# VectorE's copy of the turned rows, moved within its step in the graph layers and in the first phase

## The chip, the cores and the metric

The kernel runs on one core of one Trainium2 chip. Its time is the device time of one execution in microseconds (us). Five engines work side by side, each through its own instructions in order: TensorE (PE in the profile, with its weight loads as PEld), VectorE (DVE), ScalarE (ACT), GpSimd (POOL) and SyncE (SP). They wait for each other through semaphores.

## The reference

There are 10,000 nodes with rows of 512 numbers, and 10,000 edges sorted by their target node. The rows are normalized, go through three layers of a graph network, are added back, and go through a mixture-of-experts block with eight experts.

```python
h = layernorm(x)
for l in range(3):
    h_neigh = segment_sum(h[src], dst) / max(degree, 1)
    rst = relu(h @ W_self[l] + h_neigh @ W_neigh[l] + b[l])
    h = rst / max(norm(rst), 1e-12)
x = x + h
x = x + ffn(layernorm(x))      # top 2 of 8 experts, layer norm at the end
```

## The kernel before

Rows are worked in 79 tiles of 128. A neighbour sum is taken after the product: the kernel first computes y = h @ W_neigh and s = h @ W_self + b for every row, writes both to memory, and the next layer gathers rows of y by `src`, sums them by `dst` with a one-hot matrix on TensorE and adds s. So the work has four stages: a first phase (normalize x, multiply with the weights of layer 0), layer 1 and layer 2 (aggregate, normalize, multiply with the next weights), and a last stage (aggregate, then the expert block), which the change does not touch. The first phase also prepares the weights of all layers and the tables that place edges and nodes; that work is put between the tiles at fixed steps.

A product is made more exact by splitting h into a high part and a low part, both in 16 bits: `HH[i][:, 0, :]` is written by ScalarE (`hi0`, line 832; `hhi`, line 876), `HH[i][:, 1, :]` is the rest and is written by VectorE (line 1191; `hlo`, line 1346). TensorE turns both parts (`turn`, line 1613: eight 128 by 128 transposes into `psT`), VectorE copies them to SBUF (`turn`, line 1199, `HT`), and TensorE multiplies: `neigh` into `psY` and `own` into `psS`, twelve matmuls each (line 486). ScalarE and VectorE take y from `psY` as a high and a low part (`yhi`, line 841; `ylo`, line 1206), and VectorE takes s (`sev`, line 1216, `SB`).

The order on each engine is a list of stages with offsets: `(1, turn)` in step t means tile t+1. A step of TensorE in a layer is `neigh(t)`, `turn(t+1)`, `own(t)`, `aggregate(t+3)`; in the first phase it is the same without `aggregate`. `neigh(t)` waits for the copy of tile t (`s.ht`), and `turn(t)` waits for both parts of tile t. `HT`, `HH`, `psT`, `psY` and `psS` have two buffers each.

A step of VectorE in a layer is `one_hot(t+5)` (line 1298, `Sm`), `hlo(t+2)`, `ylo(t)`, `turn(t+1)`, `carry_lo(t+3)` (line 1307, the carry of a sum from one tile of edges to the next), `combine(t+3)` (line 1322, `R`), `sum_squares(t+3)` (line 1330), `sum_floor(t+3)` (line 1340), `sev(t)`. ScalarE computes the high part of the carry (line 857) as soon as `aggregate` is done. GpSimd raises the sum of squares to the power -1/2 (`scl`, line 728; line 656 in the first phase), and ScalarE's `hhi` uses it. GpSimd also issues the indirect transfers (lines 633, 706, 719, 735), each in its order.

In the first phase a step of VectorE is `norm0(t+2)`, `ylo(t)`, `turn(t+1)`, `stats0(t+3)`, `sev(t)`, with the preparation work ahead of `norm0`. `norm0` writes the normalized row `R` (line 1187), then waits for ScalarE's high part and writes the low part (line 1191), two instructions in one function.

Of the kernel before, what the change touches and what calls it, by code (L numbers as in the profile page):

```python
# [23 lines left out]
T = -(-E // EPT)  # L24
# [76 lines left out]
def run_steps(tiles, stages, begin, end, run=0):  # L101
    for step in range(begin, end):
        for off, f in stages:
            if 0 <= step + off < tiles:
                f(Tile(step + off, run))


def run_tiles(tiles, stages, run=0):
    offs = [o for o, _ in stages]
    run_steps(tiles, stages, -max(max(offs), 0), tiles - min(min(offs), 0), run)  # L110


def run_plan(tiles, stages, jobs, windows=()):
    offs = [o for o, _ in stages]
    begin, end = -max(max(offs), 0), tiles - min(min(offs), 0)
    cuts = sorted({begin, end} | {j[0] for j in jobs} | {e for w in windows for e in w[:2]})
    for a, b in zip(cuts, cuts[1:]):
        for at, f, arg in jobs:
            if at == a:
                f() if arg is None else f(arg)  # L120
        run_steps(tiles, stages + [(0, f) for x, y, f in windows if x <= a and b <= y], a, b)


def after(eng, sem, n):
    if n > 0:
        eng.wait_ge(sem, n)
# [101 lines left out]
def build(nc, x, src, dst, W_self, W_neigh, b, Wg, W1, b1, W2, b2, ln_g, ln_b, out_g, out_b, out):  # L228
    with ExitStack() as ctx:
# [733 lines left out]
        def _(dve):  # L963
# [218 lines left out]
            def norm0(t):  # L1182
                i = t.slot(2)
                dve.wait_ge(s.sc, (t + 1).n)
                after(dve, s.hhi, (t + -1).n)
                after(dve, s.hlo, (t + -1).n)
                dve.tensor_scalar(R[i][:, :], X[i][:, :], mv[:, i, 0:1], scl[:, i:i + 1], ALU.subtract, ALU.mult  # L1187
                                  ).then_inc(s.rr, 1)
                dve.wait_ge(s.hhi, (t + 1).n)
                dve.wait_ge(s.rr, (t + 1).n)  # L1190
                dve.scalar_tensor_tensor(HH[i][:, 1, :], R[i][:, :], LN_UP, HH[i][:, 0, :], ALU.mult, ALU.subtract  # L1191
                                         ).then_inc(s.hlo, 1)

            def turn(t, l):
                s = ph[l]
                i = t.slot(2)
                dve.wait_ge(s.tr, (t + 1).n)
                after(dve, s.sp, (t + -1).n)
                dve.tensor_copy(HT[i][:, :, :, :], psT[i][:, :, :, :]).then_inc(s.ht, 1)  # L1199

            def ylo(t, l):
                s = ph[l]
                i = t.slot(2)
                dve.wait_ge(s.yhi, (t + 1).n)
                k = Y_LN / (WUP * LN_UP) if l == 0 else Y_H / (WUP * H_UP)
                dve.scalar_tensor_tensor(YB[i][:, D:2 * D], psY[i][:, :], k, YB[i][:, 0:D], ALU.mult, ALU.subtract  # L1206
                                         ).then_inc(s.ylo, 1)

            def sev(t, l):
                s = ph[l]  # L1210
                i = t.slot(2)
                dve.wait_ge(s.sp, (t + 1).n)
                if t.t >= 2:
                    dve.wait_ge(s.s2[i], (t + -2).landed(2))
                c = C[f"s{l}"]
                dve.scalar_tensor_tensor(SB[i][:, :], psS[i][:, :], downs[:, c:c + 1], bias[:, l, :],  # L1216
                                         ALU.mult, ALU.add).then_inc(s.sev, 1)
# [44 lines left out]
            def tables():  # L1262
# [6 lines left out]
                for l in range(LAYERS):  # L1269
# [4 lines left out]

            rest = range(N_FIRST, len(NAMES))
            run_plan(TN,
                     [(2, norm0), (0, lambda t: ylo(t, 0)), (1, lambda t: turn(t, 0)), (3, stats0),
                      (0, lambda t: sev(t, 0))],
                     [(WSTEP(m) + 2, weight_norm, m) for m in rest] + [(WSTEP(m) + 3, weight_scale, m) for m in rest]
                     + [(WSTEP(m) + 4, weight_lo, m) for m in rest]  # L1280
# [12 lines left out]
            def one_hot(t, l):  # L1293

                s = ph[l]
                i = t.slot(GRING)
                after(dve, s.agg, (t + (1 - GRING)).n)
                dve.tensor_scalar(Sm[i][:, :], iota16[:, :], colT[:, t.t:t.t + 1], rowval[:, 0:1],
                                  ALU.is_equal, ALU.mult).then_inc(s.smat, 1)

            def carry_lo(t, l):
                s = ph[l]
                i, o = t.slot(2), (t + 1).slot(GRING)
                if t.t == T - 1:
                    return
                dve.wait_ge(s.chi, (t + 1).n - t.run)
                dve.scalar_tensor_tensor(G[o][0:1, D:2 * D], psA[0 if l == 3 else i][0:1, :], 1.0 / CARRY,
                                         G[o][0:1, 0:D], ALU.mult, ALU.subtract).then_inc(s.clo, 1)

            def combine(t, l):  # L1310
                s = ph[l]
                i = t.slot(2)
                if l == 1:
                    dve.wait_ge(s.x[i], t.landed(2))
                else:
                    dve.wait_ge(s.xs[i], Tile(t.t, l - 2).landed(2))
                dve.wait_ge(s.agg, (t + 1).n)
                if l == 3 and not (t.t == T - 1):

                    dve.wait_ge(s.chi, (t + 1).n - t.run)  # L1320
                after(dve, s.rr, (t + -1).n)
                dve.scalar_tensor_tensor(R[i][:, :], psA[0 if l == 3 else i][:, :], invs[:, l - 1, t.t:t.t + 1],  # L1322
                                         Sl[i][:, :], ALU.mult, ALU.add).then_inc(s.r, 1)

            def sum_squares(t, l):

                s = ph[l]
                i = t.slot(2)
                dve.wait_ge(s.r, (t + 1).n)
                dve.scalar_tensor_tensor(junk[:, :], R[i][:, :], 0.0, R[i][:, :], ALU.max, ALU.mult,  # L1330
                                         accum_out=ss[:, i:i + 1]).then_inc(s.dv2, 1)

            def sum_floor(t, l):

                s = ph[l]
                i = t.slot(2)
                dve.wait_ge(s.dv2, (t + 1).n)
                after(dve, s.sc, (t + -1).n)
                up = 1.0 if l == 3 else H_UP ** -2
                dve.tensor_scalar(ssm[:, i:i + 1], ss[:, i:i + 1], 1e-24, up, ALU.max, ALU.mult).then_inc(s.ss, 1)  # L1340

            def hlo(t, l):
                s = ph[l]
                i = t.slot(2)
                dve.wait_ge(s.hhi, (t + 1).n)
                dve.scalar_tensor_tensor(HH[i][:, 1, :], RR[i][:, :], scl[:, i:i + 1], HH[i][:, 0, :],  # L1346
                                         ALU.mult, ALU.subtract).then_inc(s.hlo, 1)

            for l in (1, 2):
                run_tiles(T, [(5, lambda t, l=l: one_hot(t, l)), (2, lambda t, l=l: hlo(t, l)), (0, lambda t, l=l: ylo(t, l)),  # L1350
                                      (1, lambda t, l=l: turn(t, l)), (3, lambda t, l=l: carry_lo(t, l)),
                                      (3, lambda t, l=l: combine(t, l)), (3, lambda t, l=l: sum_squares(t, l)),
                                      (3, lambda t, l=l: sum_floor(t, l)), (0, lambda t, l=l: sev(t, l))], l - 1)

# [407 lines left out]
```

## Time and profile before

| | us |
|---|---|
| median of 3 runs | 2334.58 (2333.9 to 2334.83) |
| the profiled execution | 2329.04 |
| its span, first to last instruction | 2327.3 |
| PE busy | 2108.8 (91%) |
| DVE busy | 1784.6 (77%) |
| POOL busy | 1253.7 (54%) |
| ACT busy | 990.4 (43%) |

The page of the profile gives the busy time of every engine, the chain of work that ended last, and the costliest groups of instructions. A matmul's end is modelled: consecutive matmuls overlap in the records, so the distance between two starts says more than a duration. Idle time of an engine is put down to the engine and line that released it.

### The profile page before, as it was taken

To read this page: it belongs to the slowest core of one execution; us is meant where nothing else is said; L and a number is where in the kernel's file an instruction comes from. 1 tells how busy PE (TensorE), PEld (TensorE's weight loads), DVE (VectorE), ACT (ScalarE), POOL (GpSimd) and SP (SyncE) were. 2 spreads that over 40 slices of the span, in tenths; PEclk is the share of its full clock that TensorE was granted. 3 is DMA by queue.
4 is the path that set the end of the run, shared out by engine and by line. 5 is a ranking of instruction groups with operands and counts; after the bars stand their busy time and mean duration, and the time that the engine had idled before them with its cause. 6 is when DMAs were issued, how large, how long until landed. Compare 5 with 4: busy or idle time off the path is not lost.

```text
span 2327.3 us, 45193 instructions
## 1 busy us (share of the span) xinstructions
PE 2108.8 (91%) x15947; PEld 1163.2 (50%) x15947; DVE 1784.6 (77%) x4201; ACT 990.4 (43%) x1698; POOL 1253.7 (54%) x1396
## 2 busy tenths in 40 slices
PE   1988889888799999999799999998389999999997
PEld 0444344334344444444344444444167777777775
DVE  4778887556587878887688787876479999999974
ACT  1222111111233333333333333332677777777761
POOL 3770003871455555554344444443658888888754
PEclk9999999999899999999899999999589999999998
DMA  4453335783355555554566666664546565565533
GB/s 129 138 153 120 109 118 132 116 114 107 121 170 163 168 167 170 163 168 144 167 206 209 211 210 205 209 212 165 158 108 143 129 138 136 129 138 135 132 49 43
DMA packets 162789, 343.48 MB, mean 148 GB/s; under 512 B 32153, under 2 KB 32327, under 8 KB 162567
## 3 DMA queue, kind: packets, MB, share of 16 engines
q0 software_dynamic: 60816, 165.43, 27.3%
q1 hardware_dynamic: 101751, 175.16, 25.5%
q8 instruction: 130, 2.13, 0.4%
q14 instruction: 92, 0.75, 0.1%
HBM read 175.81 MB, written 165.31 MB: 147 GB/s over the span
## 4 chain that ended last, share of the span: by engine, by line
PE 52%; DVE 18%; POOL 11%; issue 11%; ACT 6%; DMA 1%; DVEq 0%; POOLq 0%; ACTq 0%
PE psS L486 19%; PE psY L486 12%; PE psY L1696 9%; POOL node_info L633 4%; POOL slot_table L633 4%; DVE YB L1206 3%; DVE R L1322 3%; DVE HT L1199 3%; ACT HH L876 2%; POOL scl L728 2%; PE psT L1613 2%; DVE HH L1346 2%; PE psS L1720 1%; PE psT L1668 1%; PE psA L1653 1%
## 5 line engine op out<-in xcount | busy, mean ns | idle before, releaser
L486 PE MATMUL psY<-w_n,HT 128*128 128x512 f16 x2844 | 672.2, 387 | 82.8 <-DVE HT L1199 79.9
L486 PE MATMUL psS<-w_s,HT 128*128 128x512 f16 x2844 | 652.5, 379 | 0.0
L486 PEld LDWEIGHTS psY<-w_n,HT 128*128 128x128 f16 x2844 | 265.8, 99 | 474.7 <-DVE HT L1199 175.9
L486 PEld LDWEIGHTS psS<-w_s,HT 128*128 128x128 f16 x2844 | 268.6, 98 | 280.2
L868 ACT ACTIVATE RR<-R 128x512 f32<-128x512 f32 x237 | 149.4, 630 | 294.6 <-DVE R L1322 294.6
L735 POOL DMA_INDIRECT y_rows<-YB,poutT x158 | 161.0, 1019 | 187.9 <-DVE YB L1206 159.7
L728 POOL TENSOR_TENSOR scl<-ssm,halfpow 128x1 f32<-128x1 f32 x158 | 88.8, 562 | 286.5 <-DVE ssm L1340 286.5
L486 PE MATMUL psS<-w_w,raw 128*128 128x512 f16 x948 | 217.5, 379 | 0.0
L832 ACT ACTIVATE HH<-R 128x512 f16<-128x512 f32 x79 | 49.6, 628 | 373.1 <-DVE R L1187 373.0
L1216 DVE SCALAR_TENSOR_TENSOR SB<-psS,downs,bias 128x512 f32<-128x512 f32 x237 | 177.8, 750 | 12.1 <-PE psS L486 9.5
L1346 DVE SCALAR_TENSOR_TENSOR HH<-RR,scl,HH 128x512 f16<-128x512 f32 x158 | 118.7, 751 | 89.0 <-ACT HH L876 89.0
L1206 DVE SCALAR_TENSOR_TENSOR YB<-psY,YB 128x512 f16<-128x512 f32 x237 | 162.0, 684 | 27.5 <-ACT YB L841 27.5
L656 POOL TENSOR_TENSOR scl<-ssm,halfpow 128x1 f32<-128x1 f32 x79 | 44.6, 564 | 254.8 <-DVE ssm L1180 249.3
L1322 DVE SCALAR_TENSOR_TENSOR R<-psA,invs,Sl 128x512 f32<-128x512 f32 x237 | 173.2, 731 | 9.0 <-ACT G L857 8.0
L876 ACT ACTIVATE HH<-RR,scl 128x512 f16<-128x512 f32 x158 | 114.0, 722 | 148.9 <-POOL scl L728 148.9
L1613 PEld LDWEIGHTS psT<-iden,HH 128*128 128x128 f16 x1896 | 127.3, 99 | 78.9 <-issue 17.5
L1613 PE MATMUL psT<-iden,HH 128*128 128x128 f16 x1896 | 146.4, 221 | 19.9 <-DVE HH L1191 14.5
L1199 DVE COPY HT<-psT 128x1024 f16<-128x1024 f16 x237 | 161.1, 680 | 0.0
L706 POOL DMA_INDIRECT G<-y_rows,srcT x120 | 128.6, 1072 | 54.5 <-issue 31.3
L841 ACT ACTIVATE YB<-psY 128x512 f16<-128x512 f32 x237 | 137.5, 580 | 43.6 <-PE psY L486 43.6
L785 POOL DMA_INDIRECT out_dram<-raw,poutT x79 | 139.1, 1761 | 15.4 <-issue 14.4
L706 POOL DMA_INDIRECT area<-y_rows,srcT x117 | 128.2, 1096 | 30.8 <-issue 30.8
(280 smaller groups left out, 3680.5 us busy)
## 6 DMA issues: line engine op xcount, KB each, us to landing
self_rows<-SB SPq DMA_DIRECT2D x236, 256.0 KB, 2.0
Sl<-self_rows SPq DMA_DIRECT2D x158, 256.0 KB, 3.5
X<-in_x_dram SPq DMA_DIRECT2D x78, 256.0 KB, 2.8
y_rows<-YB SPq DMA_DIRECT2D x78, 256.0 KB, 2.2
out_dram<-obb SPq DMA_DIRECT2D x78, 256.0 KB, 4.2
raw<-in_L_gnn_W_neigh_dram SPq DMA_DIRECT2D x12, 256.0 KB, 4.5
raw<-in_L_gnn_W_self_dram SPq DMA_DIRECT2D x12, 256.0 KB, 4.8
y_rows<-YB,poutT POOLq DMA_INDIRECT x158, 3.0
```

Source lines behind the costliest of these rows:

```text
L486: mm = eng.matmul(acc, lhs[:, a, c, :], w[:, bpart, c, :], start=(n == 0), stop=(stop and n == 3 * KC - 1))
L633: pool.indirect_dma_start(to[:, :], bass.IndirectOffsetOnAxis(ap=index[0:rows, k:k + 1], axis=0), value[0:rows, k, :], None, bounds_check= ...
L706: pool.indirect_dma_start(G[i][:, :], None, Yd[l - 1][:, :], bass.IndirectOffsetOnAxis(ap=srcT[:, t.t:t.t + 1], axis=0), bounds_check=node ...
L735: pool.indirect_dma_start(Yd[l][:, :], bass.IndirectOffsetOnAxis(ap=poutT[:, t.t:t.t + 1], axis=0), YB[i][:, :], None, bounds_check=node_l ...
L876: act.activation(HH[i][:, 0, :], RR[i][:, :], ACT.Copy, scale=scl[:, i:i + 1]).then_inc(s.hhi, 1)
L1199: dve.tensor_copy(HT[i][:, :, :, :], psT[i][:, :, :, :]).then_inc(s.ht, 1)
L1206: dve.scalar_tensor_tensor(YB[i][:, D:2 * D], psY[i][:, :], k, YB[i][:, 0:D], ALU.mult, ALU.subtract).then_inc(s.ylo, 1)
L1216: dve.scalar_tensor_tensor(SB[i][:, :], psS[i][:, :], downs[:, c:c + 1], bias[:, l, :], ALU.mult, ALU.add).then_inc(s.sev, 1)
L1322: dve.scalar_tensor_tensor(R[i][:, :], psA[0 if l == 3 else i][:, :], invs[:, l - 1, t.t:t.t + 1], Sl[i][:, :], ALU.mult, ALU.add).then_in ...
L1346: dve.scalar_tensor_tensor(HH[i][:, 1, :], RR[i][:, :], scl[:, i:i + 1], HH[i][:, 0, :], ALU.mult, ALU.subtract).then_inc(s.hlo, 1)
L1613: mm = pe.transpose(psT[i][:, a, c, :], HH[i][:, a, c * P:(c + 1) * P], iden16[:, :])
L1696: pe.matmul(psH[:, cols], w[:, bpart, c, cols], h[:, a, c, :], start=first, stop=False)
```

## The change

In the first phase, the low part of `norm0` becomes a stage of its own, `lo0`, and `turn` runs between the two. In layers 1 and 2, `turn` runs ahead of `hlo` and `ylo`. No instruction is added or removed, and the semaphores and their counts stay.

```diff
--- before.py
+++ after.py
@@ -1186,6 +1186,9 @@
                 after(dve, s.hlo, (t + -1).n)
                 dve.tensor_scalar(R[i][:, :], X[i][:, :], mv[:, i, 0:1], scl[:, i:i + 1], ALU.subtract, ALU.mult
                                   ).then_inc(s.rr, 1)
+
+            def lo0(t):
+                i = t.slot(2)
                 dve.wait_ge(s.hhi, (t + 1).n)
                 dve.wait_ge(s.rr, (t + 1).n)
                 dve.scalar_tensor_tensor(HH[i][:, 1, :], R[i][:, :], LN_UP, HH[i][:, 0, :], ALU.mult, ALU.subtract
@@ -1274,7 +1277,7 @@
 
             rest = range(N_FIRST, len(NAMES))
             run_plan(TN,
-                     [(2, norm0), (0, lambda t: ylo(t, 0)), (1, lambda t: turn(t, 0)), (3, stats0),
+                     [(2, norm0), (1, lambda t: turn(t, 0)), (2, lo0), (0, lambda t: ylo(t, 0)), (3, stats0),
                       (0, lambda t: sev(t, 0))],
                      [(WSTEP(m) + 2, weight_norm, m) for m in rest] + [(WSTEP(m) + 3, weight_scale, m) for m in rest]
                      + [(WSTEP(m) + 4, weight_lo, m) for m in rest]
@@ -1347,8 +1350,8 @@
                                          ALU.mult, ALU.subtract).then_inc(s.hlo, 1)
 
             for l in (1, 2):
-                run_tiles(T, [(5, lambda t, l=l: one_hot(t, l)), (2, lambda t, l=l: hlo(t, l)), (0, lambda t, l=l: ylo(t, l)),
-                                      (1, lambda t, l=l: turn(t, l)), (3, lambda t, l=l: carry_lo(t, l)),
+                run_tiles(T, [(5, lambda t, l=l: one_hot(t, l)), (1, lambda t, l=l: turn(t, l)),
+                                      (2, lambda t, l=l: hlo(t, l)), (0, lambda t, l=l: ylo(t, l)), (3, lambda t, l=l: carry_lo(t, l)),
                                       (3, lambda t, l=l: combine(t, l)), (3, lambda t, l=l: sum_squares(t, l)),
                                       (3, lambda t, l=l: sum_floor(t, l)), (0, lambda t, l=l: sev(t, l))], l - 1)
```

## Rows read from the trace of the kernel before

**Rows 1.** Windows of line 1613 alone: window, us, PE and PEld busy (count), clock, DMA, GB/s.

```profile
622.15:1094.46 472.31, 45.74 (x601) 39.80 (x600) 1.00 0.51 165
...
58.77:161.63 102.86, 9.83 (x128) 8.56 (x128) 1.00 0.50 143
161.63:402.62 240.99, 21.75 (x280) 18.99 (x280) 0.96 0.38 123
```

**Rows 2.** Timeline of layer 1: start us, us, engine, line, operation.

```profile
1025.40 0.61 PE L1613 MATMUL psT<-iden,HH 128*128 128x128 f16 x8
...
1031.46 0.61 PE L1613 MATMUL psT<-iden,HH 128*128 128x128 f16 x8
...
1032.55 0.30 DVE L1298 TENSOR_SCALAR Sm<-iota,colT,rowval 128x128 f16<-128x128 f16 x1
...
1034.71 0.38 PE L1654 MATMUL psA<-G,Sm 128*128 128x512 f16 x1
...
1038.00 0.61 PE L1613 MATMUL psT<-iden,HH 128*128 128x128 f16 x8
```

**Rows 3.** The chain of waits in layer 1: start us, us, what.

```profile
1030.30 0.74 DVE R L1322
...
1033.40 0.52 DVE HH L1346
...
1034.07 0.68 DVE YB L1206
1034.75 0.61 DVE HT L1199
1035.40 2.76 PE psY L486 x12
...
1042.90 0.74 DVE R L1322
```

**Rows 4.** Windows, all engines: PE, PEld, DVE, ACT, POOL busy (count), clock, DMA, GB/s.

```profile
650.00:750.00 100.00, 98.23 (x542) 46.23 (x541) 80.08 (x161) 38.39 (x64) 58.09 (x64) 1.00 0.52 166
58.77:161.63 102.86, 95.47 (x529) 45.42 (x528) 76.12 (x149) 30.52 (x38) 80.73 (x79) 1.00 0.50 143
161.63:402.62 240.99, 215.94 (x1157) 102.79 (x1156) 198.72 (x625) 49.91 (x77) 36.85 (x52) 0.96 0.38 123
402.62:519.25 116.63, 98.60 (x545) 46.17 (x544) 69.00 (x136) 18.96 (x34) 94.16 (x84) 1.00 0.82 115
```

**Rows 5.** Waits between 161.63 and 402.62 us: total us, times, longest.

```profile
DVE HH L1191 <- ACT HH L832: 27.1, 35, 2.1
...
PE psY L486 <- DVE HT L1199: 22.1, 13, 4.9
```

**Rows 6.** Timeline of VectorE in the first phase, at 344 us.

```profile
344.16 0.54 DVE L1187 TENSOR_SCALAR R<-X,mv,scl 128x512 f32<-128x512 f32 x1
...
346.60 0.68 DVE L1199 COPY HT<-psT 128x1024 f16<-128x1024 f16 x1
...
349.99 0.54 DVE L1187 TENSOR_SCALAR R<-X,mv,scl 128x512 f32<-128x512 f32 x1
```

**Rows 7.** Waits of POOL between 402.62 and 519.25 us.

```profile
POOL slot_table L633 <- issue: 20.0, 65, 1.9
```

**Rows 8.** Timeline of VectorE at the start of layer 1.

```profile
608.85 0.31 DVE L1298 TENSOR_SCALAR Sm<-iota,colT,rowval 128x128 f16<-128x128 f16 x1
...
611.04 0.68 DVE L1199 COPY HT<-psT 128x1024 f16<-128x1024 f16 x1
```

**Rows 9.** Windows of two steps of the first phase, columns as in Rows 4.

```profile
259.00:267.33 8.33, 5.79 (x33) 2.71 (x32) 7.15 (x31) 1.12 (x2) 0.55 (x1) 1.00 0.27 94
303.19:315.55 12.36, 7.48 (x33) 3.14 (x32) 10.31 (x34) 1.74 (x3) 0.55 (x1) 0.86 0.25 84
```

**Rows 10.** Timeline of PE late in the first phase.

```profile
538.16 5.30 PE L486 MATMUL psY<-w_n,HT 128*128 128x512 f16 x12 [4.96 <-DVE HT L1199]
```

**Rows 11.** Waits of PE between 640 and 1094 us.

```profile
PE psY L486 <- DVE HT L1199: 6.4, 26, 0.3
```

## The prediction

> **What bounds the kernel now.** I first cut the span into its stages by windows that count the transposes, eight of which belong to a tile [rows 1]: layer 1 holds 75 steady steps (600 transposes) in 472.31 us, 6.297 us a step, and layer 2 as many in 472.32 (its row, from 1137.77 us, repeats the first). The first phase has one stretch of 16 steps in 102.86 us (6.43 a step) and one of 35 in 240.99 us (6.89). The last stage is not touched.
>
> Second, what a step costs TensorE when it waits for nothing. In a layer the distance between the transposes of two tiles alternates: 1031.46 - 1025.40 = 6.06 us, then 1038.00 - 1031.46 = 6.54 us [rows 2]. Both steps hold the same 24 products, 8 transposes and 2 aggregation matmuls. In the long one the second aggregation matmul starts at 1034.71 [rows 2], and the next product could start one matmul spacing later: twelve matmuls take 1038.00 - 1035.40 = 2.60 us, 0.217 each, so at 1034.93. It starts at 1035.40 [rows 3], 0.47 late, which is the 0.48 by which the long step is longer. So 6.06 is TensorE's own pace, and mean 6.30 minus 6.06 is lost.
>
> Third, the chain of waits says why [rows 3]. It runs from `R` at 1030.30 through POOL's `scl`, ScalarE's high part, VectorE's low part of h (1033.40), `ylo` (1034.07), the copy to HT (1034.75), the product (1035.40), own and aggregation, and arrives at an `R` again at 1042.90: 12.60 us for two steps, just 2 x 6.30. The reader is to see that this is a closed loop that paces both layers, and that the copy is in it behind two VectorE instructions that it does not need.
>
> In the first phase VectorE is the bound where it has preparation work: in the 35 steps it is busy for 198.72 us [rows 4] and waits 27.1 us in 35 waits for ScalarE's high part [rows 5], 0.77 us each; together with the gaps between instructions this is nearly the whole 240.99. An ordinary step of this stretch takes 5.83 us from `R` to `R` (349.99 - 344.16), and the copy starts 2.44 us after `R` [rows 6]. TensorE's own pace here is the layer's without two matmuls, 6.06 - 2 x 0.217 = 5.63.
>
> In the slot-table stretch from 402.62 to 519.25 POOL is busy for 94.16 us [rows 4] and in 20.0 us more it issues transfers [rows 7]: 114.2 of 116.6, so POOL sets the pace there.
>
> **The change, part by part.** No instruction is added, so each engine's busy time stays; only waits can go or come.
>
> *Layers, the copy.* `one_hot` starts at 1032.55 and takes 0.30, so VectorE can reach the copy at 1032.85. The transposes that it needs started at 1031.46 and took 0.61, done at 1032.07 [rows 2]: no wait, 0.78 us in hand. The copy then runs from 1032.85, not 1034.75 [rows 3], 1.90 us earlier. The loop of 12.60 shrinks to 10.70 for two steps, under TensorE's 12.12. TensorE becomes the bound and the step becomes 6.06. Per layer 75 x (6.297 - 6.06) = 17.8 us, both layers 35.5. As ends I keep 30 (a step of 6.10) and 36.
>
> *Layers, what moves back.* The copy takes about 0.61 us of VectorE's time and now fills the 0.55 us between `one_hot` and the low part, 1032.85 to 1033.40 [rows 2, 3], in which VectorE waited for ScalarE's high part; `hlo` starts some 0.13 us later than now, `ylo` too. Behind them VectorE waits for the carry, so this costs nothing as long as it has idle time: it is busy 80.08 us in 100 [rows 4], and a step of 6.06 leaves about 0.9 us. `ylo` later by 0.13 also holds back POOL's issue of the y rows by as much; POOL is busy 58.09 in 100 [rows 4] and reaches `scl` with time in hand. SP's queue stores `SB` and loads the next rows in the same order as before. What is late next is nothing but TensorE.
>
> *Layers, the start.* In the first steps of a layer the copy waits behind `hlo` of the next tile, which waits for POOL and ScalarE: `Sm` ends at 608.85 + 0.31 = 609.16 and the copy starts at 611.04 [rows 8]. Now it starts at about 609.2, and the first product 1.9 us earlier; two layers, 3.8 us (ends 0 and 3.8).
>
> *First phase, 161.63 to 402.62.* After `R`, VectorE waited about 0.70 us for the high part; the copy fills that. The round of 5.83 falls by 0.61 to 0.66, to 5.2, under TensorE's 5.63. The most that VectorE can give back over 35 steps is 35 x 0.66 = 23 us, and some 2 us of waits on slow products: 25. The least is to count only the steps in which TensorE is recorded waiting for the copy, 13 [rows 5], x 0.66 = 9. The truth lies between, since a step that is now bound by TensorE gives nothing itself but lets VectorE get ahead. That lead counts in heavy steps: a copy that starts 1.2 to 1.9 us earlier leaves more work behind it that may run beside the next product. In the heavy step of 12.36 us VectorE is busy 10.31 and TensorE's clock is 0.86, so that 7.48 us are spent on what takes 5.79 in the step of 8.33 us at full clock [rows 9]; a shorter wait may save part of this 1.7 us, which occurs in about five steps. I take 17.
>
> *First phase, POOL's stretches.* In the 17 steps before 519.25 nothing is gained. In the 16 steps before 161.63 POOL is busy for 80.73 us [rows 4] with the same pattern of four transfers and their gaps, so I take 2 us (0 to 3.5), mostly from its start.
>
> *First phase, the end.* The product at 538.16 starts after a wait of 4.96 us for the copy [rows 10], which follows `R` by the chain of high part, low part and `ylo`. The copy now follows `R` after 0.57 instead of 2.44 [rows 6], 1.9 us; I take 2 (0 to 4).
>
> Sum: 35.5 + 3.8 + 17 + 2 + 2 = 60.3 us. The profiled execution took 2329.04, 5.5 less than the median 2334.58 of the runs shown; 2329.04 - 60.3 = 2268.7, and beside the median runs 2334.58 - 60.3 = 2274.3. The lowest sum is 30 + 9 = 39 (2296), the highest 36 + 3.8 + 25 + 3.5 + 4 = 72 (2262).
>
> **The rivals.**
>
> *The recorded idle time is all there is.* TensorE's waits for the copy add up to only 6.4 us in layer 1 [rows 11], and it is busy 98.23 us in 100 [rows 4]. If the records are right about what is free, the layers give 2 x 6.4 = 13 us, and with 21 of the first phase and 4 of the starts the kernel lands at 2334.6 - 38 = 2297. Against it: equal steps of 6.06 and 6.54 differ by 0.48 while the recorded wait is at most 0.3, since a recorded matmul of 0.38 us overlaps the next one. The Trainium skill, "Perfetto Trace Analysis", section "Identifying the Most-Contended Engine", says the same of this row: matmul busy share is no good measure of the distance to the roofline. By that rule the row's 1.8% free is not the limit of the gain; the step distances here agree.
>
> *The layers give all, the first phase nothing*, because its preparation work or POOL sets the end of each stretch: 39 us, 2295. For it: POOL's stretch. Against it: the 27.1 us of waits [rows 5].
>
> *Another loop takes over in the layers.* Sum of squares, `scl`, high part, low part and the turn of the next tile is a loop as well. If it held 6.30, only the first phase would gain: 21 us, 2313. Against it: the low part ends near 1034.1, and TensorE turns that tile at 1038.00 [rows 2], almost 4 us later.
>
> *Slower: the copy blocks VectorE's queue.* Behind the copy stand `hlo`, `ylo`, the carry, `combine`, and behind those POOL and ScalarE. If the transposes end later than `one_hot`, all wait. The transposes have 0.78 us in hand in the long step and about 0.3 in the short one, and 0.9 us of idle time follows; from 1.2 us of lateness on, every further bit lengthens the step. At 0.3 us net a step over 150 steps this is +45, with the first phase's gain 2334.6 + 45 - 21 = 2359. Against it: TensorE no longer starts its step late, so the transposes come earlier, not later.
>
> *The copy is not what releases TensorE* and nothing changes, 2334.
>
> **How the numbers follow.** The forecast has 0.70, the recorded idle time 0.08, the first phase nothing 0.09, another loop 0.06, no change 0.03, slower 0.04. The predicted time is 2274.3. The forecast's own range is 2262 to 2296; with the next two rivals it is 2262 to 2300, which leaves out 0.13 and some of the forecast's own tails. A change under 0.2% (4.7 us) could not be told from none by such runs; the chances are faster 0.93, same 0.03, slower 0.04.
>
> **What would show it right or wrong.** In the layers the distance between two tiles' transposes is 6.06 throughout without alternation, TensorE no longer waits for HT, and VectorE's wait for the high part (L1346) is gone while its wait for the carry (L1307) has grown; both steady stretches last about 454.5 us. In the first phase the wait at L1191 is near 0, the step of 5.83 is 5.63, the POOL stretch still takes 6.8 us a step, and the 35 steps take about 224 us. The forecast is wrong if a step of the layers stays above 6.15, if VectorE is seen waiting for the transposes in most steps, or if POOL's `scl` comes later relative to the aggregation.

## The result and the profile after

The kernel after took 2276.45 us in the median of four runs (2271.36 to 2279.31), against 2334.7 us for the kernel before (four runs, 2333.9 to 2335.96). The ratio is 0.9754, with a 95% interval of 0.9739 to 0.9769; 58.2 us less. Timed again later, beside other runs of the kernel before (median 2341.25 us), the same kernel gave 0.9755 (0.9739 to 0.9772). The profiled executions took 2329.04 and 2276.38 us, 52.7 apart: that of before was a short one, that of after a middling one.

Where the 52.7 us went is read from the distances of the transposes, as for the kernel before. All 75 steady steps of layer 1 take 454.37 us now, where [rows 1] has 472.31. The same window view of line 1616, which is line 1613 moved by three lines (columns: window, us, PE and PEld busy with counts, clock, DMA, GB/s):

```profile
605.93:1060.30 454.37, 45.73 (x600) 39.80 (x600) 1.00 0.52 171
```

The chain of waits in the same stretch has lost everything but TensorE, where [rows 3] went through ScalarE, VectorE and POOL (start us, us, what):

```profile
1012.00 0.45 PE psT L1616 x8
1012.45 2.59 PE psS L486 x12
1015.03 0.22 PE psA L1656
1015.25 0.22 PE psA L1657
1015.47 2.59 PE psY L486 x12
1018.06 0.45 PE psT L1616 x8
```

From one group of transposes to the next is 6.06 us, in every step.

The kernel before was less regular than the prediction took it to be. Its steps alternate between 6.06 and 6.54 us only from about 1000 us on. At the start of layer 1 they take 6.53 and 6.07 us, then the two come closer, and about the middle both take 6.30 us. What stays is the sum of two neighbouring steps, 12.58 to 12.61 us through both layers. These lines of the kernel before are from the middle (columns as [rows 2]):

```profile
798.57 0.61 PE L1613 MATMUL psT<-iden,HH 128*128 128x128 f16 x8
...
801.82 0.38 PE L1654 MATMUL psA<-G,Sm 128*128 128x512 f16 x1
802.27 2.76 PE L486 MATMUL psY<-w_n,HT 128*128 128x512 f16 x12
...
804.87 0.61 PE L1613 MATMUL psT<-iden,HH 128*128 128x128 f16 x8
...
811.17 0.61 PE L1613 MATMUL psT<-iden,HH 128*128 128x128 f16 x8
```

Here the product starts 0.45 us behind the second aggregation matmul, where one spacing is 0.217; it is 0.23 us late in every step, and the record lists no wait at all. So the round of two tiles is fixed, and how its 12.60 us are split between the two is not.

VectorE's timeline of the step at 1012.00 us of the kernel after shows the copy right behind `Sm`, the low part behind the copy without a wait, and the idle time now ahead of the carry:

```profile
1012.93 0.30 DVE L1301 TENSOR_SCALAR Sm<-iota,colT,rowval 128x128 f16<-128x128 f16 x1
1013.15 0.68 DVE L1202 COPY HT<-psT 128x1024 f16<-128x1024 f16 x1
...
1013.78 0.75 DVE L1349 SCALAR_TENSOR_TENSOR HH<-RR,scl,HH 128x512 f16<-128x512 f32 x1
1014.45 0.68 DVE L1209 SCALAR_TENSOR_TENSOR YB<-psY,YB 128x512 f16<-128x512 f32 x1
...
1016.12 0.68 DVE L1310 SCALAR_TENSOR_TENSOR G<-psA,G 1x512 f16<-1x512 f32 x1 [0.99 <-ACT G L857]
```

VectorE's waits between 610 and 1060 us (total, times, longest) say the same of all steps:

```profile
DVE area L1310 <- ACT area L857: 37.2, 37, 1.0
DVE G L1310 <- ACT G L857: 36.9, 37, 1.0
...
DVE HH L1349 <- ACT HH L876: 0.2, 1, 0.2
```

The windows of all engines answer to [rows 4] (columns as there). TensorE is recorded as busy all the time in the layer; POOL's stretch, the last row, is no shorter per step:

```profile
650.00:750.00 100.00, 100.00 (x560) 49.23 (x558) 81.80 (x164) 40.08 (x67) 60.90 (x67) 1.00 0.54 175
157.30:388.32 231.02, 213.80 (x1156) 104.01 (x1157) 199.32 (x628) 49.50 (x77) 38.12 (x54) 0.96 0.40 128
388.32:507.55 119.23, 101.77 (x545) 47.36 (x544) 68.79 (x136) 18.96 (x34) 93.48 (x85) 0.96 0.87 113
```

In the first phase the step is TensorE's. VectorE's timeline, against [rows 6]: `R` to `R` is 5.62 us, not 5.83, the copy starts 1.02 us behind `R`, not 2.44, and it now waits for the transposes:

```profile
342.64 0.54 DVE L1187 TENSOR_SCALAR R<-X,mv,scl 128x512 f32<-128x512 f32 x1
343.66 0.69 DVE L1202 COPY HT<-psT 128x1024 f16<-128x1024 f16 x1 [0.48 <-PE psT L1616]
...
348.26 0.54 DVE L1187 TENSOR_SCALAR R<-X,mv,scl 128x512 f32<-128x512 f32 x1
```

The waits of VectorE over the same 35 steps answer to [rows 5]. The 27.1 us for the high part are 3.0, and a new wait of 14.2 us stands where VectorE has time:

```profile
DVE HT L1202 <- PE psT L1616: 14.2, 19, 3.3
DVE R L1187 <- POOL scl L656: 4.2, 3, 2.0
DVE HH L1194 <- ACT HH L832: 3.0, 2, 1.5
```

### The profile page after: what moved, and what is told of

Read it like the earlier page. It is cut to its first block, busy times and chain, and to the rows that moved or that the text cites. A ratio compares the mean times of both kernels' runs of the same rounds, so it can differ in the third digit from the quotient of the medians.

```text
span 2274.7 us, 45187 instructions
## 1 busy us (share of the span) xinstructions
PE 2088.6 (92%) x15941; PEld 1178.0 (52%) x15947; DVE 1773.4 (78%) x4201; ACT 991.2 (44%) x1698; POOL 1253.7 (55%) x1396
## 4 chain that ended last, share of the span: by engine, by line
PE 77%; POOL 8%; DVE 6%; issue 6%; ACT 2%; DMA 1%; SPq 0%; DVEq 0%; POOLq 0%; ACTq 0%
PE psS L486 30%; PE psY L486 22%; PE psY L1699 9%; POOL slot_table L633 4%; PE psT L1616 4%; PE psA L1656 2%; PE psA L1657 2%; POOL node_info L633 2%; PE psS L1723 2%; PE psT L1671 1%; PE psA L486 1%; PE psY L1709 1%; PE psY L1701 1%; PE psA L1733 1%; POOL scl L656 1%
## 5 line engine op out<-in xcount | busy, mean ns | idle before, releaser
L486 PEld LDWEIGHTS psY<-w_n,HT 128*128 128x128 f16 x2844 | 279.6, 99 | 402.4 <-DVE HT L1202 60.0
L735 POOL DMA_INDIRECT y_rows<-YB,poutT x158 | 160.9, 1019 | 188.7 <-DVE YB L1209 160.4
L1202 DVE COPY HT<-psT 128x1024 f16<-128x1024 f16 x237 | 162.2, 685 | 41.3 <-PE psT L1616 39.8
L785 POOL DMA_INDIRECT out_dram<-raw,poutT x79 | 139.1, 1760 | 15.4 <-issue 14.4
L486 PEld LDWEIGHTS psS<-w_w,raw 128*128 128x128 f16 x948 | 89.5, 98 | 93.3
```

The costliest lines, as they stand in the source:

```text
L486: mm = eng.matmul(acc, lhs[:, a, c, :], w[:, bpart, c, :], start=(n == 0), stop=(stop and n == 3 * KC - 1))
L735: pool.indirect_dma_start(Yd[l][:, :], bass.IndirectOffsetOnAxis(ap=poutT[:, t.t:t.t + 1], axis=0), YB[i][:, :], None, bounds_check=node_l ...
L785: pool.indirect_dma_start(out[:, :], bass.IndirectOffsetOnAxis(ap=poutT[:, t.t:t.t + 1], axis=0), OUT[i], None, bounds_check=node_limit, o ...
```

## The experiments

Each kernel was timed beside runs of the kernel before on its chip, whose median moved between 2332.8 and 2342.4 us; so times are compared with those, and stretches by their profiles.

### Only the layers, and only the first phase

```diff
 e1_layers_only: the diff of the layers alone
 e2_first_only: the diff of the first phase alone (norm0, turn, lo0, ylo)
```

> The new order in layers 1 and 2 only; the first phase as before. Theory (a closed loop of 12.60 us for two tiles paced the layers, TensorE's own 6.06 us paces them now): both steady stretches fall from 472.3 to 454.4 us as in the kernel after, and with the starts of the layers the time is 2334.7 - 38.6 = 2296 us. Rival (the gain of the layers depends on the state in which the first phase leaves the queues and memory): less than 30 us.

> The new order in the first phase only; the layers as before. If the parts add up, the first phase gives what the whole change gave less the layers: 15 us by the two traces (last transposes of the phase at 584.1 and 568.9 us), or 58.2 - 38.6 = 20 us by the medians, so 2315 to 2320 us, with the alternation of 6.06 and 6.54 us in the layers as before. Rival (the first phase gives nothing, POOL and preparation set its end): 2334 us.

The layers alone gave 2293.03 against 2332.83, ratio 0.9831 (0.981 to 0.9851), 39.8 us. The first phase alone gave 2309.95, ratio 0.9906 (0.9884 to 0.9928), 22.9 us. Their sum, 62.7, agrees with the 58.2 of the whole within these intervals. The first is the 38.6 that was expected, the second is more than the 15 to 20. In the first kernel the last transposes of the first phase start at 584.6 us and those of layer 2 at 1577.7, 993.1 later, against 1031.6 before: 38.5 us. In the second the layers keep 6.297 us a step and the first phase ends 20.4 us earlier (563.7 for 584.1). Both parts act by themselves.

### The copy behind the low part

```diff
-[one_hot, (2, hlo), (0, ylo), (1, turn), carry_lo, ...]
+[one_hot, (2, hlo), (1, turn), (0, ylo), carry_lo, ...]     # e3: layers only
-[(2, norm0), (0, ylo), (1, turn), (3, stats0), (0, sev)]
+[(2, norm0), (1, turn), (0, ylo), (3, stats0), (0, sev)]    # e4: first phase only
```

> Layers only, and the copy only ahead of ylo: one_hot, hlo, turn, ylo; first phase as before. Theory of the closed loop: ylo's 0.68 us leaves the loop of 12.60 us, which becomes 11.92 for two tiles, under TensorE's 12.12; so half of the move gives the whole gain of the layers, 36 to 39 us, 2296 to 2299 us, steps of 6.06 us. Rival (each of the two instructions passed gives its share of the gain, in proportion to 0.68 of 1.90 us): 14 us, 2321 us.

> First phase only, and the copy only ahead of ylo: norm0 with its wait and the low part, turn, ylo; layers as before. VectorE still waits 0.7 us for the high part in each step, so its round of 5.83 us stays and only the copy comes 0.6 us earlier. Theory (what the first phase gained came from filling VectorE's wait): 0 to 7 us, 2328 to 2335 us. Rival (what counts is that the copy is ahead of ylo): most of the first phase's 15 to 20 us.

In the steady steps of the layers half of the move is enough: 2298.16 against 2332.83, ratio 0.9854 (0.9836 to 0.9873), 34.7 us. The windows of line 1613:

```profile
622.87:1077.24 454.37, 45.75 (x600) 39.80 (x600) 1.00 0.53 171
```

This is the same 454.37 us to the last digit. The 5.1 us that separate this kernel from the one with the whole move in the layers (2293.03) are not in these stretches. About 3 of them are at the starts of the layers: from the first transposes of a layer to its steady steps it takes 15.2 and 15.5 us, against 14.4 and 13.4 there and 15.3 and 15.1 in the kernel before. Behind the low part the copy gains nothing at a start. VectorE still waits for the high part in every step (waits from 640 to 1076 us):

```profile
DVE HH L1346 <- ACT HH L876: 38.2, 72, 0.8
DVE G L1307 <- ACT G L857: 14.8, 36, 0.4
```

So it was not this wait that cost time, but that it stood in the loop; out of the bound, 38.2 us of it cost nothing. The first phase is the opposite case. With the wait kept, the kernel takes 2325.5 us, ratio 0.9967 (0.9952 to 0.9982), 7.3 us less and a third of what the whole move gives there. The 35 steps from 160.9 us take 241.2 us, as before (241.0), and the waits for the high part in them are the same 27.1 us in 35. There VectorE was full, and only time given back to VectorE counts. Where its 7.3 us lie is open. Its profile ends the phase 2.6 us earlier, by the last nine steps (61.4 us for 64.9), but these take anything from 61.7 to 65.9 us in the five profiles with the old order there (before, e1, e3, e5, e8).

### Less work for TensorE, in both orders

```diff
-products(pe, psS[i], HT[i], WT[f"s{l}"])
+products(pe, psS[i], HT[i], WT[f"s{l}"], parts=((0, 0), (0, 1), (1, 0))[:3 if l == 0 else 2])
```

> The order before, with less work for TensorE: own in layers 1 and 2 leaves out the four products of the low part of h (8 matmuls instead of 12; the result is less exact). TensorE's own pace falls by 4 x 0.216 = 0.87 us to 5.19 us a tile. Theory of the closed loop: the loop holds one own for two tiles, so it falls from 12.60 to 11.73 us, 5.87 us a tile, 0.43 less: 2 x 75 x 0.43 = 64 us, about 2269 us, and TensorE now waits for the copy in every step. Rival (TensorE was the bound in the layers already): 0.87 us a tile, 130 us.

> The order after, with the same four products left out. Theory (after the change TensorE alone paces the layers): 6.06 - 0.87 = 5.19 us a tile if nothing else is near; VectorE's round of busy time is about 5.1 us plus a wait for the carry, so it may take over between 5.2 and 5.7 us. Against the kernel after that is 50 to 130 us less. Rival (the loop still sets the pace at 6.06): under 10 us less.

In the order before, the windows of line 1613 give 440.25 / 75 = 5.870 us a step, as the theory of the loop foretold:

```profile
636.34:1076.59 440.25, 45.74 (x601) 39.81 (x601) 1.00 0.54 177
```

The chain of waits of that kernel has the same links as [rows 3], and takes 811.02 - 799.30 = 11.72 us for two tiles, 0.88 us under 12.60, because its one `own` has four matmuls fewer (1.73 us, not 2.59):

```profile
799.30 0.74 DVE R L1322
...
803.05 0.68 DVE YB L1206
803.73 0.61 DVE HT L1199
...
804.39 2.76 PE psY L486 x12
807.15 0.45 PE psT L1613 x8
807.60 1.73 PE psS L486 x8
...
811.02 0.74 DVE R L1322
```

TensorE's waits between 640 and 1076 us rise from 6.4 us in 26 waits [rows 11] to one in every step:

```profile
PE psY L486 <- DVE HT L1199: 37.0, 74, 1.2
```

In the order after, the same cut gives 389.62 / 75 = 5.195 us, the expected 5.19 of TensorE alone:

```profile
612.44:1002.06 389.62, 389.62 (x2251) 194.96 (x2250) 373.26 (x751) 181.29 (x300) 269.76 (x296) 1.00 0.61 200
```

VectorE is then busy for 373.26 of 389.62 us and still does not set the pace. The same cut is worth 0.43 us a step in one order and 0.86 in the other: that is the difference between a loop and an engine as the bound. The times, of two runs each, are 2275.26 (ratio 0.9717, 0.9689 to 0.9746; 67 us less than before, 64 expected) and 2149.28 (0.9179, 0.9153 to 0.9206). The second is 135 us under the kernel after on the same chip (2284.75, e12 below), a little over the 50 to 130 expected.

### More work for VectorE, in both orders

```diff
+for more in spare if t.t >= 6 else ():      # behind one_hot, two tiles
+    dve.tensor_scalar(more, iota16, colT[:, t.t:t.t + 1], rowval[:, 0:1], ALU.is_equal, ALU.mult)
```

> The order after, with two more instructions of the size of one_hot (0.30 us each) behind it in every step of layers 1 and 2 and the last stage, written to tiles nobody reads. The prediction held that VectorE has 0.9 us to spare in a step of 6.06 us. If so, 0.6 us more leaves the layers at 6.06 us a tile. Rival (VectorE is as good as full after the change): 6.06 us rises by up to 0.6 us, 90 us over both layers. The last stage is a thing of its own and may grow; the layers are read from the distances of the transposes.

> The order before with the same two added instructions. Theory of the closed loop: one_hot does not lie on the chain that was followed (the chain goes from scl over ScalarE's high part), and VectorE waited 0.55 us behind it for that high part, so the first 0.55 us are covered and the rest enters the loop: 12.60 + 0.05 to 0.10 us for two tiles, 6.32 to 6.35 us a tile. Rival (all VectorE work between R and the copy is in the loop): 12.60 + 0.60 = 13.20, 6.60 us a tile.

In the order after, the layers do not notice it. The wait for the carry falls from 1.0 us to 0.6, and the windows of its line 1620 give:

```profile
611.44:1065.81 454.37, 45.74 (x600) 39.80 (x600) 1.00 0.53 171
```

In the order before they do not either. The expectation of 6.32 to 6.35 us was a little too high: the windows of its line 1617 give 472.30 us, 6.297 a step.

```profile
632.82:1105.12 472.30, 45.74 (x600) 39.80 (x600) 1.00 0.51 165
```

Its timeline shows why: the two instructions overlap and are over by 854.95, and the low part starts at 855.04, when the high part is there. The whole addition fits in the old wait.

```profile
854.20 0.30 DVE L1299 TENSOR_SCALAR Sm<-iota,colT,rowval 128x128 f16<-128x128 f16 x1
854.42 0.53 DVE L1302 TENSOR_SCALAR spare<-iota,colT,rowval 128x128 f16<-128x128 f16 x2
855.04 0.75 DVE L1350 SCALAR_TENSOR_TENSOR HH<-RR,scl,HH 128x512 f16<-128x512 f32 x1
```

The whole kernels took 2286.68 and 2346.79 us (ratios 0.9766 and 1.0022). The added instructions run in the last stage as well, which takes 5.6 to 6.2 us more in both profiles (718.5 and 717.8 us from the last transposes of layer 2, where the kernels after and before take 712.8 and 711.6).

### What is left in the first phase

```diff
 e9: run_plan(..., ahead=2): VectorE's preparation work behind norm0 and turn of its step
 e10:
-STEP_TABLES = 71
+STEP_TABLES = 76
-columns(slotT, ndT, table, slot_limit, NF, i, g.t * 4, 4)
+columns(slotT, ndT, table, slot_limit, NF, i, g.t * 3, min(3, 80 - g.t * 3))   # 27 steps
 e11: both.   e12: the kernel after, unchanged
```

> The kernel after, and in the first phase VectorE's preparation work stands behind norm0 and the copy of its step instead of ahead of them. What is left of the heavy steps (11.5, 8.9, 10.6, 10.2, 11.1 us against 5.63) is a copy that waits for preparation work. Theory: the copy is then in time, and TensorE waits only when the low part of the next tile comes too late, one product (2.6 us) later than the copy is due, less the 0.6 us of the copy itself; about 1 to 2 us less in each of 6 heavy steps, 5 to 10 us, 2266 to 2271 us. Rival (VectorE's sum of work sets these steps, wherever the work stands): within 3 us of the kernel after.

> The kernel after, and GpSimd puts 3 columns of the slot table per step instead of 4, over 27 steps instead of 20, the table's loading moved from step 71 to 76. POOL's round in this stretch falls from 6.77 us by one transfer of 1.49 us to about 5.3, under TensorE's 5.63. Theory (POOL alone sets the pace from step 53 to 69, the change gave nothing there): 16 steps x 1.14 = 18 us less, and fewer stalls of POOL's queue: 2253 to 2262 us. Rival (the stall at the end grows by what is gained, since the table is ready later): within 5 us of the kernel after.

> Both of these together. If they act in different stretches, their gains add: 23 to 28 us under the kernel after, about 2250 us.

> The kernel after again, unchanged. In its first profile the first phase had two stalls that the kernel before did not show: TensorE waited 2.4 us for the weights w1 before step 18, and POOL stood still twice between 440 and 482 us. If these are chance, the second profile shows the phase ending at another time than 568.9 us, between 563 and 578 us as in the other kernels with the new order, with the 35 steps before the slot table again taking 222 to 223 us.

| | median us | ratio to before | 18-52 | 52-69 | 69-78 |
|---|---|---|---|---|---|
| before | 2341.25 | | 231.1 | 116.6 | 64.9 |
| e12, after again | 2284.75 | 0.9755 | 214.8 | 128.7 | 64.6 |
| e9 | 2291.37 | 0.9792 (0.9775 to 0.9808) | 221.8 | 129.8 | 62.2 |
| e10 | 2262.1 | 0.9665 (0.9647 to 0.9683) | 216.8 | 105.6 | 62.3 |
| e11 | 2266.55 | 0.9686 (0.9668 to 0.9703) | 221.0 | 107.3 | 61.1 |

The last columns are us between the transposes of these steps of the first phase, counted from 0; the row of before has them from its first profile.

The preparation work behind the copy was a miss, 7 us slower. In it TensorE waits elsewhere (waits from 171.34 to 393.14 us):

```profile
PE psA L1571 <- ACT sq L811: 7.6, 1, 7.6
PE psY L491 <- DVE HT L1207: 6.7, 6, 1.2
PE psT L1621 <- issue: 3.8, 2, 2.3
PE psT L1621 <- ACT HH L837: 3.1, 2, 2.1
```

The waits for the copy did fall, from 11.5 us in the kernel after to 6.7. But two others take more than that back. ScalarE's squares wait for a piece of this preparation work, and TensorE has sums over them ahead of its product; this wait grew from 3.0 us to 7.6. And in four steps, 6.9 us in all, TensorE waits ahead of its transposes, where it did not in the kernel after: at 279.70 us it starts them as soon as the low part is done (279.60), which stands behind preparation work. What was moved late was itself on the path. The expectation had named the second wait and priced it too low.

Three columns a step is faster than both kernels: 2262.1 against 2284.75 of the kernel after on the same chip, 22.7 us less, and 79 less than before. Expected were 14 to 23 us. The windows of its 17 steps (columns as [rows 4]):

```profile
387.89:493.51 105.62, 98.03 (x545) 47.83 (x544) 69.44 (x135) 18.88 (x33) 68.83 (x66) 0.98 0.97 127
```

POOL is busy for 68.83 of 105.62 us now. The first seven of these steps take 5.63 us, TensorE's pace, where the kernels before and after have 6.77 in most. This shows that POOL's round was the bound there. But the 17 steps take 6.2 us each on average, because POOL then waits for its own transfers to land, with the DMA engines busy for 0.97 of the stretch on average (waits of POOL from 387.89 to 493.51 us):

```profile
POOL slot_table L635 <- DMA slot_table<-area: 22.7, 12, 4.9
```

Both together (e11) were a miss: 18.2 us under the kernel after where 23 to 28 were expected, since most of the loss of e9 stayed (4.5 us against e10).

The second profile of the kernel after ended its first phase at 578.7 us, not 568.9, just outside the 563 to 578 expected, with the 34 steps from 18 to 52 again short (214.8 us; from 18 to 53 it is 220.5, where 222 to 223 were expected) and the slot-table stretch longer. There POOL waits for its own transfers to land (waits from 385.32 to 514.04 us):

```profile
POOL slot_table L633 <- issue: 23.8, 64, 5.9
POOL slot_table L633 <- DMA slot_table<-area: 10.4, 4, 5.7
```

In the profile of before that second wait is 1.1 us in two. These 17 steps took 116.6 to 130.7 us in the six profiles of kernels with the old order or half of the move in the first phase (before, e1, e3, e4, e5, e8) and 117.1 to 129.8 us in six with the new one (after, e2, e6, e7, e9, e12): the stalls come with either order. They hide more or less of the gain from one profile to the next, and what triggers one was not found.

## Why the prediction was right

It gave 2274.3 us, and 2276.45 was measured: 58.2 us less where 60.3 were forecast. The mechanism and the largest term were right. That the total is only 2 us off is partly luck. The two profiles differ by 52.7 us; the other 5.5 are there because the profiled execution of before was a short one, and where they lie is open. The terms of the first phase were off by up to 7 us, in both directions.

- **The loop in the layers, 35.5 us.** Shown. The profiles give 2 x 17.95 = 35.9 us. The step is 6.06 throughout, and the wait at the low part has turned into one at the carry. That it was a loop of two tiles, and not VectorE's load or TensorE's, is shown by the cut in `own` (11.72 us for two tiles) and by the half move (the same 454.37 us). The steady alternation on which the prediction read it holds only for the end of the layer; the 6.06 us of TensorE was right, and so was the mean.
- **What moves back, nothing.** Shown. VectorE kept 0.99 us ahead of the carry (0.9 was expected), and 0.5 us more work in each step did not move the pace. From the second aggregation matmul to POOL's `scl` it is 3.38 us in both kernels (1034.71 to 1038.09 before, 1015.09 to 1018.47 after), so `scl` does not come later.
- **The starts of the layers, 3.8 us.** The step was right, its size too large: 1.0 and 1.7 us. The copy does start earlier, at 593.80, 2.16 us behind the transposes at 591.64, where it was 4.14 us (611.04 [rows 8] less 606.90). But the first product behind it then takes 5.30 us, not 4.48:

```profile
594.54 5.30 PE L486 MATMUL psY<-w_n,HT 128*128 128x512 f16 x12 [1.04 <-DVE HT L1202]
```

The line of the kernel before is this one:

```profile
611.78 4.48 PE L486 MATMUL psY<-w_n,HT 128*128 128x512 f16 x12 [3.01 <-DVE HT L1199]
```

  The granted clock was 0.50 from 591 to 600 us, the level of 1.2 GHz, so for the whole of the product. During the product of before it was 0.50 up to 614.00 us and 0.69 on average from there to 616.10, so part of that one ran at 2.4 GHz. The time gained at the start of the product was partly lost in it.
- **The 35 steps with preparation work, 17 us.** Mis-sized in this profile: 240.99 - 231.02 = 10.0 us. In four other profiles with the new order (e2, e6, e7, e12) they took 227.9 to 229.1 us, 12 to 13 us less than 241.0. The mechanism is as predicted (high-part waits 27.1 to 3.0 us), and from step 18 on the gain is 231.1 - 216.8 = 14.3 us: 6.1 in the six longest steps (64.4 to 58.3 us) and 8.2 in the 28 others, whose mean fell from 5.95 to 5.66 us. The 5.83 us that the prediction called ordinary was one of several lengths; many steps already took TensorE's 5.63 and had nothing to give. What was missed stands in the first of the 35: TensorE arrives 4.3 us earlier and finds the weights `w1` not loaded.

```profile
162.87 5.40 PE L1553 MATMUL psA<-raw,bmat 128*128 128x512 f32 x8 [2.37 <-DMA raw<-in_L_ffn_W_dram]
```

  In the kernel before these eight matmuls follow without a wait and take 3.60 us; the wait, and slower matmuls behind it, ate nearly all of the 4.3 us. The granted clock was 0.68 on average in 162.80 to 168.20 us, so partly at the level of 1.2 GHz and partly at 2.4; TensorE had been busy for 0.23 of the 2.60 us before. In the kernel before it was 1.00 in the same window. Other profiles with the new order have the wait too: 1.99 us in e12, with 5.40 us for the eight matmuls, and 0.61 us in e2, with 3.70.
- **POOL's stretches and the end, 2 and 2 us.** The first gave 4.3 us by step 17 (1.4 at its start and 2.9 in the 16 steps), more than the 3.5 kept as its upper end. The slot-table stretch took 2.6 us more instead of nothing; a loss had not been allowed for, and by the scatter given above it may be chance, since the profile of before has the shortest stretch of its order. The last nine steps gave 3.6 us, within the 4, but not by the step that was forecast. The wait for the copy ahead of that product, 4.96 us [rows 10], grew to 6.36 us (7.7 in e2 and 6.1 in e12), and its step took 13.78 us where it was 13.25:

```profile
525.12 4.38 PE L486 MATMUL psY<-w_n,HT 128*128 128x512 f16 x12 [6.36 <-DVE HT L1202]
```

  So this reading of [rows 10] was wrong, and that the term came out near its size was luck. What all profiles with the new order share is step 74, 5.63 us for 6.8; the rest is in step 69, which takes 6.8 to 11.8 us in profiles with the old order.
- **Together** the first phase gave 15.3 us in the profile of after, 20.4 in that of e2 and 22.9 by the medians of e2, where 21 were forecast. The last stage took 1.2 us longer in the profile of after than in that of before, which no step explains.

Of the rivals, that the recorded idle time is all there is (13 us in the layers) fell most clearly: TensorE waited 6.4 us by the records in layer 1, and 17.9 came back. That the first phase gives nothing was refuted by e2 (22.9 us). The other loop did not take over: with TensorE cut to 5.19 us a tile the loops still stay below it. The copy in VectorE's queue did wait for the transposes in the first phase, 14.2 us in 19 waits over 35 steps. Taken by its words this is one of the prediction's signs of being wrong ("in most steps"), but the 35 steps got shorter, so it did not cost what this rival feared. In the layers no such wait is listed.

## What to carry to other kernels

Where steps of equal work differ in length but two neighbours always add up to the same sum, or where all take longer than the engine needs, follow the chain of waits until it closes on itself, and look in it for instructions that stand there only by their place in a queue; moving one out gains up to the next bound and not its own time. To see whether a loop or an engine sets the pace, cut the engine's work: the loop gives back its share once a round, the engine gives back all. An engine that arrives earlier may find a transfer that was hidden so far: look at what each later step waits for before adding the gains up.

## What was not expected of the hardware

The recorded wait of TensorE understated the lost time: between 640 and 1094 us it had 6.4 us in 26 waits, while the 75 steps of layer 1 lost 17.9 us. The recorded matmul takes 0.38 us and the next can start 0.217 us after it, so the first 0.16 us of each lateness are hidden; in the middle of the layer, where each product was 0.23 us late, no wait was listed. The two added instructions of 0.30 us took 0.53 us together.
